# A fused attention, recurrence and MLP kernel: opening and last stage reordered without meetings, maxima transfers issued by ScalarE

## What is computed

```
# layer 0: 16 heads of 16, cross attention, gated
a = layernorm(ctx);  Q, K, V = x @ Wq.T, a @ Wk.T, a @ Wv.T
x = x + tanh(gate) * softmax(mask(Q K^T * 16**-0.5)) V @ Wo.T
# layer 1: a recurrence over the sequence (not touched)
# layer 2: 32 query heads of 8 on 8 key heads, then layernorm
x = layernorm(softmax(Q K^T / sqrt(8) + mask) V @ Wo + bo + x)
# layer 3: two cross attentions (16 heads of 128), then the MLP
x = x + cross1(ln(x), ctx);  x = x + cross2(ln(x), ctx)
x = x + gelu(ln(x) @ fc1 + b1) @ fc2 + b2        # 256 -> 1024 -> 256
```

## Time and profile before

| | us |
|---|---|
| median of 3 runs | 1370.39 (1368.31 to 1372.71) |
| the profiled execution, as a whole | 1370.92 |
| its span, first to last instruction | 1368.9 |
| TensorE busy | 1241.1 (91%) |
| VectorE busy | 806.6 (59%) |
| ScalarE busy | 533.6 (39%) |
| GpSimd busy | 182.9 (13%) |

### The profile page before, as it was taken

The page is one execution under the profiler, slowest core; times in us unless marked ns, Lnnn a source line. Parts: engine busy times, 40 slices in busy tenths (PEclk is TensorE's granted clock), DMA queues, the critical chain, the costliest instruction groups (busy, mean ns, idle before and its releaser), DMA issues.

```text
span 1368.9 us, 18207 instructions
## 1 busy us (share of the span) xinstructions
PE 1241.1 (91%) x6176; PEld 888.1 (65%) x6176; DVE 806.6 (59%) x2372; ACT 533.6 (39%) x1223; POOL 182.9 (13%) x403
## 2 busy tenths in 40 slices
PE   4448999999999868999999699999999999999988
PEld 3135766575757533444443388888888888888877
DVE  3313547585858536677786566666666666666521
ACT  2023563334343422445555333434333434344332
POOL 3112214021212211012010200000000000000000
PEclk9568999999999978999999899999999999999999
DMA  5954703202020344342434551220303030500000
GB/s 164 237 171 106 201 3 114 108 17 101 23 100 24 109 158 138 140 149 79 151 137 139 199 193 48 76 97 28 123 1 124 1 123 1 185 1 1 1 0 31
DMA packets 106699, 130.19 MB, mean 95 GB/s; under 512 B 6897, under 2 KB 84881, under 8 KB 104369
## 3 DMA queue, kind: packets, MB, share of 16 engines
q1 hardware_dynamic: 106608, 129.05, 29.2%
HBM read 78.80 MB, written 49.94 MB: 94 GB/s over the span
## 4 chain that ended last, share of the span: by engine, by line
PE 80%; DMA 6%; SPq 5%; DVE 2%; POOL 2%; ACT 2%; issue 1%; POOLq 0%; DVEq 0%; ACTq 0%
PE J L2377 8%; PE TT L2385 8%; PE J L2395 8%; PE S L2351 4%; PE TT L2361 4%; PE OO L1047 4%; PE OO L1051 4%; PE OO L2351 4%; SPq L2642 2%; PE J L323 2%; PE J L1051 2%; PE J L1047 2%; PE OO L2589 2%; PE OO L1899 2%; PE J L1313 2%; PE S L1047 2%
## 5 line engine op out<-in xcount | busy, mean ns | idle before, releaser
L2453 ACT ACTIVATE PT<-TT 128x512 f32<-128x512 f32 x128 | 76.4, 597 | 283.1 <-PE TT L2361 283.1
L2524 DVE TENSOR_SCALAR QK<-J,cols 128x256 f32<-128x256 f32 x126 | 61.0, 484 | 71.1 <-PE J L2377 71.1
L2488 POOL COPY On<-probs 128x8 f32<-128x8 f32 x128 | 29.1, 227 | 476.6 <-DVE probs L2513 447.3
L2513 DVE TENSOR_SCALAR probs<-probs,inv 128x257 f32<-128x257 f32 x256 | 79.1, 352 | 4.5
L2361 PE MATMUL TT<-ident,probs 128*128 128x128 f32 x512 | 77.4, 274 | 1.7 <-DVE probs L2513 1.7
L1047 PE MATMUL OO<-weights_a,ctxT 128*128 128x512 f32 x136 | 70.5, 644 | 6.9 <-ACT weights_a L1062 4.0
L951 DVE CUSTOM_DVE_ANT_0 mask_b<-S,weights_a 128x256 f32<-128x256 f32 x64 | 24.6, 422 | 87.0 <-PE S L628 86.8
L2361 PEld LDWEIGHTS TT<-ident,probs 128*128 128x128 f32 x512 | 64.1, 141 | 15.7 <-DVE probs L2513 2.8
L2519 DVE COPY km<-TT 128x256 f32<-128x256 f32 x128 | 54.2, 424 | 31.0 <-PE TT L2385 30.7
L1051 PE MATMUL OO<-ctxT,weights_a 128*128 128x512 f32 x136 | 66.1, 608 | 5.0 <-SPq L307 3.0
L2505 DVE TENSOR_REDUCE maxes<-S 128x1 f32<-128x257 f32 x128 | 48.4, 420 | 30.8 <-PE S L2351 30.8
(11 more groups left out here) (392 smaller groups left out, 2740.5 us busy)
## 6 DMA issues: line engine op xcount, KB each, us to landing
wide_values<-weights_a SPq DMA_DIRECT2D x64, 256.0 KB, 2.0
wide_keys<-weights_a SPq DMA_DIRECT2D x64, 256.0 KB, 2.1
query_parts<-weights_a SPq DMA_DIRECT2D x48, 192.0 KB, 2.8
weights_a<-wide_keys SPq DMA_DIRECT2D x16, 512.0 KB, 7.0
weights_a<-wide_values SPq DMA_DIRECT2D x16, 512.0 KB, 8.4
early<-wide_keys SPq DMA_DIRECT2D x16, 512.0 KB, 8.2
early<-wide_values SPq DMA_DIRECT2D x16, 512.0 KB, 8.7
key_parts<-weights_a SPq DMA_DIRECT2D x24, 192.0 KB, 2.9
```

The source lines that it names most:

```text
L2453: act.activation(PT[:, n % 2, :], T0[:, :], ACT.Copy).then_inc(pt3_ready, 1)
L2513: ins = dve.tensor_scalar(P_[n % 2][:, qt, :], P_[n % 2][:, qt, :], inv[:, qt, n % 32:n % 32 + 1], None, ALU.mult)
L2524: dve.tensor_scalar(QK[:, n % 2, 0, 0:S], J0[:, 0:S], head_cols(f"bq{a + 1}")[:, h:h + 1], float(DIM3) ** -0.5, ALU.add, ALU.mult).then_in ...
```

## The change

- **Stores and spreads of the keys.** Each half of the key parts is stored once (`key_parts0` loses a dimension): 2 transfers of 192 KB a batch in place of 6. `spread0` reads each of them three times over with `to_broadcast`, a source of [3 copies, 24 rows, 2048] with a step of zero outermost. A spread is now two key and two query transfers of 288 KB in place of one and one of 576 KB.
- **SP's order.** `ctxT` and `rows` are loaded before the first stores (`load_first`); the mask's loads stand behind those of `ctx` and `x`; the spreads of steps 2 and 3 are issued in the loop, behind the first and second copy of the maxima; the 21 other loads of `load_rest` are issued two at a time at `i` = 6 and 7 of each step.
- **Maxima.** ACT issues the transfer itself, behind its copy and a wait for the copy's end, in layer 0 and in layer 2 (8 each).
- **Splits.** DVE instead of POOL splits the queries of batches 0 and 1 (`split0`).
- **The first instructions.** DVE's memsets stand behind the first `centre_a`, over the same bytes as half as many elements; ACT waits for `cols` alone; TensorE waits for `w0` with the key and query weights, and for `w0_vo` before the values.
- **MLP.** No meetings. `hidden` and the inputs have two buffers, `fc2` of batch b and `fc1` of batch b + 1 stand in turn on TensorE, the bias is added into `x_tok` ahead of time, one DVE add ends a batch, and SP stores each batch by itself.

```diff
         def keep_keys0(sp, b):
             sp.wait_ge(keys0_split, b + 1)
             for s in range(2):
-                for a in range(PARTS):
-                    sp.dma_start(key_parts0[b, s, a].rearrange("c p n -> p c n"),
-                                 parts0["k"][:, :, s * S:(s + 1) * S]).then_inc(key0_kept, 16)
+                sp.dma_start(key_parts0[b, s].rearrange("c p n -> p c n"),
+                             parts0["k"][:, :, s * S:(s + 1) * S]).then_inc(key0_kept, 16)
...
         def spread0(sp, m):
 
-            b, half = m // 2, m % 2
+            b, first = m // 2, m % 2 * HEADS_AT
             if m >= 4:
                 sp.wait_ge(st0_done, CHUNKS0 * (m - 3))
-            for rows_, dram, kept_ in ((k_rows0, key_parts0, key0_kept), (q_rows0, query_parts0, query0_kept)):
-                sp.wait_ge(kept_, 16 * 2 * PARTS * (b + 1))
-                sp.dma_start(rows_[m % 4][0:ROWS0, :, :, :],
-                             dram[b].rearrange("s a c (d h) n -> (a c d) s h n", d=HALF0)
-                             [:, :, half * HEADS_AT:(half + 1) * HEADS_AT, :]).then_inc(rows0_landed[m % 4], 16)
-
-        def max_rows0_sp(sp, m):
-            sp.wait_ge(max0_rows_ready, m + 1)
-            sp.dma_start(q_rows0[m % 4][ROWS0:ROWS0 + PARTS, 1, :, :], max_rows0).then_inc(max0_landed, 16)
-
-        def stacked0_sp(sp, load_rest, load_values):
-
+            here = slice(first * S, (first + HEADS_AT) * S)
+            n_here = HEADS_AT * S
+            sp.wait_ge(key0_kept, 16 * 2 * (b + 1))
+            for s in range(2):
+                sp.dma_start(k_rows0[m % 4][0:ROWS0, s, :, :],
+                             key_parts0[b, s].rearrange("c (d h) n -> (c d) (h n)", d=HALF0)[:, here]
+                             .unsqueeze(0).to_broadcast([PARTS, PARTS * HALF0, n_here]))\
+                    .then_inc(rows0_landed[m % 4], 16)
+            sp.wait_ge(query0_kept, 16 * 2 * PARTS * (b + 1))
+            for s in range(2):
+                sp.dma_start(q_rows0[m % 4][0:ROWS0, s, :, :],
+                             query_parts0[b, s].rearrange("a c (d h) n -> (a c d) (h n)", d=HALF0)[:, here])\
+                    .then_inc(rows0_landed[m % 4], 16)
+
+        def split0(eng, n, ready, done_sem, turn, step_sem, at):
+
+            eng.wait_ge(ready, turn)
+            exact, rest, parts = exact0[n], rest0[n], parts0[n]
+            eng.tensor_tensor(rest, exact, parts[:, 0, :], ALU.subtract).then_inc(step_sem, 1)
+            eng.wait_ge(step_sem, at + 1)
+            eng.tensor_copy(parts[:, 1, :], rest).then_inc(step_sem, 1)
+            eng.wait_ge(step_sem, at + 2)
+            eng.tensor_tensor(parts[:, 2, :], rest, parts[:, 1, :], ALU.subtract).then_inc(done_sem, 1)
+
+        def stacked0_sp(sp, load_first, load_rest, load_values):
+
+            load_first()
+            keep_keys0(sp, 0)
+            keep_queries0(sp, 0)
             sp.wait_ge(ones0_ready, 1)
-            for b in (0, 1):
-                keep_keys0(sp, b)
-                keep_queries0(sp, b)
-                spread0(sp, 2 * b)
-                spread0(sp, 2 * b + 1)
-            load_rest()
+            spread0(sp, 0)
+            spread0(sp, 1)
+            keep_keys0(sp, 1)
+            keep_queries0(sp, 1)
             for at in range(-LEAD0, LAST0):
                 n, i = at // CHUNKS0, at % CHUNKS0
                 b = n // 2
                 if i == 5 and 0 <= n + 1 < STEPS0:
-                    max_rows0_sp(sp, n + 1)
+                    if n < 1:
+                        sp.wait_ge(max0_rows_ready, n + 2)
+                        spread0(sp, n + 3)
+                if n >= 0 and i >= 6:
+                    load_rest(4 * n + 2 * (i - 6), 4 * n + 2 * (i - 6) + 2)
...
                     if m >= 1:
                         act.wait_ge(max0_landed, 16 * m)
                     act.activation(max_rows0, O1[0:PARTS * HEADS_AT, 0:S], ACT.Copy).then_inc(max0_rows_ready, 1)
+                    act.wait_ge(max0_rows_ready, m + 1)
+                    act.dma_start(q_rows0[m % 4][ROWS0:ROWS0 + PARTS, 1, :, :], max_rows0).then_inc(max0_landed, 16)
...
                 fetch_x(0, J0)
-                act.wait_ge(loaded["const"], 16 * 3)
+                act.wait_ge(loaded["cols"], 16)
                 fetch_a(0, O1)
...
-                for rows_ in k_rows0:
-                    ins = dve.memset(rows_[:, 1, :, :], 1.0)
-                ins.then_inc(ones0_ready, 1)
                 dve.wait_ge(loaded["ctx_first"], 16)
                 statistics(0)
                 centre_a(0)
+                for i in range(4):
+                    ins = dve.memset(weights_a[:, 5120 + i * 2048:6144 + i * 2048], BF16_ONES)
+                ins.then_inc(ones0_ready, 1)
...
+                def widen(b, i):
+                    project(pe, banks[i], lambda k, o: fc1[:, k, (2 * i + o) * P:(2 * i + o + 1) * P],
+                            inputs[b % 2], 2, fc1_done)
+
+                def narrow(b, m):
+                    pe.wait_ge(gelu_ready, n_hidden * b + m + 1)
+                    for t in range(TQ):
+                        mm = pe.matmul(outs[b % 2][:, t * S:(t + 1) * S], hidden[b % 2][:, m, t * P:(t + 1) * P],
+                                       fc2[:, m, :], start=(m == 0 and t == 0), stop=(m == n_hidden - 1 and t == TQ - 1))
+                    if m == n_hidden - 1:
+                        mm.then_inc(fc2_done, 1)
+
+                def flip_input(b):
+                    pe.wait_ge(xn5_ready, b)
+                    if b >= 2:
+                        pe.wait_ge(h5_ready, b - 1)
+                    flip(pe, T0, xn, h5_flipped)
+
                 pe.wait_ge(loaded["fc"], 16 * 2)
-
-                def main(b, following, b_next):
-                    for i, bank_ in enumerate(banks):
-                        project(pe, bank_, lambda k, o: fc1[:, k, (2 * i + o) * P:(2 * i + o + 1) * P],
-                                hT[:, :, 0:S], 2, fc1_done)
-                    front_pe(following, pe, T0, None)
-                    for m in range(FF // P):
-                        pe.wait_ge(gelu_ready, m + 1)
-                        for t, bank_ in enumerate((O0, O1)):
-                            mm = pe.matmul(bank_[:, 0:C], hidden[:, m, t * P:(t + 1) * P], fc2[:, m, :],
-                                           start=(m == 0), stop=(m == FF // P - 1))
-                    mm.then_inc(fc2_done, 1)
-
-                batches(pe, "pe", 5, main)
+                for i in range(len(banks)):
+                    widen(0, i)
+                flip_input(1)
+                for b in range(B):
+                    if b >= 2:
+                        pe.wait_ge(mlp_out, b - 1)
+                    for i in range(len(banks)):
+                        narrow(b, 2 * i)
+                        narrow(b, 2 * i + 1)
+                        if b + 1 < B:
+                            if i == 0:
+                                pe.wait_ge(h5_ready, b + 1)
+                            widen(b + 1, i)
+                        if i == 1 and b + 2 < B:
+                            flip_input(b + 2)
...
-            lead(sp, B - 1)
-            store(0, (B - 1) * TQ)
-            lead(sp, 1)
-            store((B - 1) * TQ, B * TQ)
-            sp.wait_ge(stored, 16 * 2)
+            mlp_sp(sp, store)
```

165 lines of the change are left out of this document (85 added, 80 removed).

## The result

| | us |
|---|---|
| before, median of 4 runs | 1370.89 |
| after, median of 4 runs | 1356.01 (1353.58 to 1359.06) |
| ratio after / before | 0.990, 95% interval 0.988 to 0.992 |
| the profiled execution after, and its span | 1357.32, 1355.3 |

The change makes the kernel faster by 14.9 us, 1.1%, about half of the 28.7 that I forecast. The measured time is 14 us above the predicted 1342, and 4 us above the 1332 to 1352 that I gave for this case. The side was right and the size was not.

A forecast was written before the change was run, and what follows sets the result against it. TensorE bounds the kernel (80% of the span), so only stages where it idles can give: 23.1 us from the first layer plus 5.6 from the MLP, 28.7 in all, 1370.4 to 1342; this case 1332 to 1352, overall 1314 to 1374.

The forecast's parts named there:

- The first instructions: Opening: statistics start at 3.5 us instead of 9.34, `aT` at 8 instead of 16.5, keys at 9.2 instead of 17.68.
- the fills: Opening: TensorE's fills start at 37.5 us, once the first spread has landed; before, 43.27.
- Three engines: First layer: the key spread's outermost count of 3 leaves three DMA engines, 8.0 us a step, some 75 GB/s.
- The fourth spread's wait: First layer: fourth spread's rows land at 85.3 us, due at 78.2; TensorE waits 7.1, plus 2.7 of half clock.
- The grouped-query layer: 530 to 780 us: no gain, between -1 and +8 if ScalarE's issues of the maxima are exposed.
- the MLP: Last stage: three gaps between batches go, 5.0, and 0.6 at the end: 5.6 us, between 4.5 and 6.
- `at` = 0 starts at: First layer's first transposed scores start at 54 us instead of 84.65, so the opening gives 30.6.
- waits of TensorE behind it: First layer: TensorE waits for key rows at third, fourth, fifth and seventh spread: 4.5, 7.1, 2.1 and 4.0 us.
- and 2.7 of half clock: First layer: a long wait costs 2.7 us more at half clock; charged at the fourth and seventh spread.
- The rival of twelve engines: A compiler folds the broadcast, `at` = 0 starts at 48.5 and nothing stalls behind it: 1315 us; chance 0.12.
- 3.04 us after the issue they have landed.: Opening: ScalarE copies the maxima near 51 us; they land 3.04 after issue, so `at` = 0 starts at 54.
- maxima held up on ScalarE's path: Rival: maxima late at `at` = 0, 8 and 16, mostly beside the rows' waits: + 8, 1350 us; chance 0.08.

The follow-up runs named there:

- experiment 1: Changed kernel with the key rows' three copies made by a zero step inside ([24 rows, 3 copies]) and query rows in the same order: 1330.6 us, ratio 0.972.
- the second execution: The changed kernel itself, unaltered, profiled once more: 1355.4 us.
- Experiments 8 and 11: 8: changed kernel, layer 0's maxima issued by SP: 1369.2 us. 11: inner copies, early spreads, queries split first, step 3's spread and value weights awaiting maxima: 1316.8 us.
- kernels with inner copies: Changed kernel with the key broadcast's zero step inside, 1330.6 us, and kernels built on it with early spreads, 1330.7, or further reordering, down to 1316.8.

## Why the prediction was right and wrong

Right, with their sizes:

- **The first instructions** and the fills (38.74 for 37.5).
- **Three engines.** Share 0.19, 76 GB/s, 8 us a step; priced at 27 us (1342 against the rival's 1315), measured 25.4 (experiment 1). The term that was to eat the gain did so in the size given. The Trainium skill ("DMA: Bandwidth & Descriptors", "Why a DMA increments its semaphore by 16 and not by 1") states the rule for the number of engines; both orders of the same broadcast agree with it, 0.19 of the engines with [3, 24] outermost and 0.86 (stores among them) with [24, 3].
- **The fourth spread's wait**: 85.3 forecast with `at` = 0 at 54; it came at 90.93 with `at` = 0 at 59.86, the same distance to 0.3 us. That closeness is luck: the forecast had 17.2 us to SP's store of the keys, 4.5 of them a wait for the third spread that never came, and 14.1 from there; the trace has 14.4 and 16.7. And TensorE, not held by the third spread, waited 10.19 there and not 7.1.
- **The grouped-query layer** at nothing; **the MLP** at 5.6, between 4.5 and 6: measured 6.5. The term is small by 0.9. A slip is in it: 16.2 - 14.4 is 1.8, so three gaps are 5.4 and the sum is 6.0. And TensorE's own busy time fell too, from 57.6 to 56.8, which I had not counted on.

Wrong, in the first layer, 7.9 us (to `at` = 40) where 23.1 were forecast:

| step of the forecast | forecast | measured | adds |
|---|---|---|---|
| `at` = 0 starts at | 54 | 59.86 | +5.9 |
| waits of TensorE behind it (forecast: all for rows; measured: one for rows, two for maxima) | 4.5 + 7.1 + 2.1 + 4.0 = 17.7 | 10.19 + 2.21 + 2.65 = 15.1 | -2.6 |
| loss at half clock behind it | 2.7 x 3 = 8.1 | 46.2 us at half clock = 23.1 | +15.0 |
| the rest (1.0 of it: the groups of the earlier trace rows were cleared of 2.7 for each of two stretches that cost 3.2; the other 2.1 was not traced) | | | -3.1 |
| sum | | | +15.2 |

Windows of the kernel before, from the end of its second and third wait for maxima to where the clock rose again, columns as in the earlier trace rows:

```profile
103.82:110.33 6.51, 6.51 (x38) 3.66 (x39) 2.54 (x13) 2.01 (x4) 2.43 (x4) 0.50 0.00 0
124.46:130.81 6.35, 6.35 (x37) 3.80 (x38) 2.16 (x9) 1.98 (x3) 0.78 (x4) 0.50 0.59 139
```

1. **The step that failed most is "and 2.7 of half clock" behind each long wait** (and 2.7 in the first group). I took it from a stretch that I put at 5.4 us by a window of 5.0 inside of it. Already in the kernel before, the stretches behind the two waits were 6.5 and 6.4 us long, a loss of 3.2 each (the two rows above). In the changed kernel the four stretches behind `at` = 0 are 9.6, 9.3, 6.8 and 20.5 us long. I had also given half clock to two of four waits only; every wait from 2.2 us on was followed by one, but for the one at 140.17 in the second execution. It is a term of the sum that was mis-sized, by 15 us: 8.1 forecast, 23.1 measured. The rival of twelve engines suffered from the same: I had written "nothing stalls behind it", and experiment 1 had a stall of 4.6, with 5.6 lost to half clock behind it, and came 16 above my 1315.
2. **"3.04 us after the issue they have landed."** Their last packet moved 7.0 us after the issue, and TensorE started after 7.7. Of the 5.9 us that `at` = 0 came late, 4.7 are this and 1.2 the later fills. The earlier trace rows is a transfer issued behind all of SP's bulk, as it ran out; here SP issued 1.2 MB of rows in the same moment, 52.12. The rival "maxima held up on ScalarE's path" was half true, and I had given it 0.08: they did come late at `at` = 0, 16 and 32. What I had set against it, that the rows' waits would cover it, did not hold: at `at` = 0, 16 and 32 TensorE waited for the maxima, and the rows of the third, fifth and seventh spread were there in time in that execution. That the sum of the waits came out near (15.1 for 17.7) is therefore luck. Experiments 8 and 11 show the cause.

The Trainium skill ("DMA: Bandwidth & Descriptors", "Queues, rings and completion order") says that an engine takes turns between the queues it has work for, and I had let that rule speak against the rival. The trace agrees for the last part only: between 57.0 and 59.1 us both queues move in turns, the maxima's 27 packets among 61 of SP's. But from 52.2 to 56.9 no packet of ScalarE's queue moved at all. The rule says nothing of that first part, and the measured sum decides. What holds the first packet back is not shown.

Two windows of the changed kernel's transfers around that landing, each with its packets by queue, q1 being SP's and q10 ScalarE's:

```profile
q1 hardware_dynamic: 145, 0.54, 39.7%
```

```profile
q1 hardware_dynamic: 61, 0.20, 37.2%
q10 hardware_dynamic: 27, 0.01, 2.7%
```

**What stays open:** what sets the length of a stretch at half clock. The same kernel had 20.5 and 10.2 us at one place in two executions. In kernels with inner copies the stretches behind the last waits of the layer were 3.4 to 6.8 us, but these waits stand elsewhere. A wait of 2 to 3 us was not put in by itself.
